# Cross-attention in two stages: all Q of the first batch and the split of the second x in stage one, K loaded ahead of x

## What is computed

```python
qh = _split_heads(x @ wq.T + bq, 16)
kh = _split_heads(ctx @ wk.T + bk, 16)
vh = _split_heads(ctx @ wv.T + bv, 16)
scores = einsum('ntd,nsd->nts', qh, kh) / sqrt(32) + mask * PAD
attn = softmax(scores)
out = _merge_heads(einsum('nts,nsd->ntd', attn, vh)) + x
out = (out - mean) / sqrt(var + 1e-5) * gamma + beta
```

## Time and profile before

| | |
|---|---|
| median of 3 runs | 1111.35 us (1110.16 to 1111.82) |
| profiled execution | 1110.28 us, span 1108.5 us |
| stage one | 0 to 131.4 us of the span |
| steady loop, as read below | 220 to 1000 us |
| busy | PE 97%, DVE 85%, POOL 69%, ACT 65% |

### The profile page before, as it was taken

How to read it: one execution, slowest core, us unless ns; L and a number is a source line. 1 busy time by engine, 2 the same in 40 slices (tenths; PEclk the granted TensorE clock), 3 DMA queues, 4 the chain that set the end, 5 groups by cost and what they waited for, 6 DMA issues and landing times.

```text
span 1108.5 us, 26950 instructions
## 1 busy us (share of the span) xinstructions
PE 1072.9 (97%) x7541; PEld 985.3 (89%) x7541; DVE 939.7 (85%) x1782; ACT 721.0 (65%) x1136; POOL 767.5 (69%) x668
## 2 busy tenths in 40 slices
PE   7999889999999999999999999999999999999984
PEld 6888679999999999999999999999999999999974
DVE  6888478888888888888888888888898888888895
ACT  3321266777777777777777777777777777777651
POOL 3999623576777777777777777777777777777564
PEclk9999999999999999999999999999999999999995
DMA  7754455555655655555556655665665555555443
GB/s 227 257 167 178 171 127 127 133 146 152 167 151 156 164 164 153 141 152 152 136 157 164 164 155 147 154 160 150 160 164 164 140 151 151 144 143 127 126 117 124
DMA packets 176906, 171.34 MB, mean 155 GB/s; under 512 B 110004, under 2 KB 111556, under 8 KB 176868
## 3 DMA queue, kind: packets, MB, share of 16 engines
q1 hardware_dynamic: 167044, 145.36, 45.7%
q10 hardware_dynamic: 9824, 25.50, 10.2%
HBM read 96.76 MB, written 48.85 MB: 131 GB/s over the span
## 4 chain that ended last, share of the span: by engine, by line
PE 82%; DVE 2%; issue 1%; ACT 1%; DMA 1%; SPq 0%; POOL 0%; DVEq 0%; POOLq 0%; ACTq 0%
PE q_ps L811 32%; PE o_ps L859 23%; PE t_ps L845 12%; PE s_ps L831 11%; PE s_ps L834 3%; DMA x_rows<-in_x 1%; PE q_ps L859 1%; SPq L729 0%; DVE attn L950 0%; ACT q_a L1142 0%; DVE stats L919 0%; ACT q_b L1144 0%; POOL attn L1064 0%; DVE row_max L985 0%; ACT pt L1159 0%
## 5 line engine op out<-in xcount | busy, mean ns | idle before, releaser
L859 PE MATMUL o_ps<-v_tiles,pt 128*128 128x66 f32 x2520 | 312.9, 272 | 0.3 <-DVE attn L911 0.3
L859 PEld LDWEIGHTS o_ps<-v_tiles,pt 128*128 128x128 f32 x2520 | 304.3, 193 | 0.5 <-issue 0.5
L1159 ACT COPY pt<-t_ps 128x512 f32<-128x512 f32 (+1 forms) x320 | 186.6, 583 | 159.7 <-PE t_ps L845 156.6
L1096 POOL TENSOR_TENSOR x_lo<-xT_raw,x_hi 128x512 fp32r<-128x512 f32 x124 | 158.2, 1277 | 189.1 <-ACT x_hi L1132 188.6
L985 DVE TENSOR_REDUCE row_max<-s_ps 128x8 f32<-128x616 f32 x256 | 204.7, 800 | 90.0 <-PE s_ps L834 79.1
L1122 ACT ACTIVATE probs<-probs 128x616 f32<-128x616 f32 x256 | 184.3, 720 | 82.3 <-DVE probs L994 74.7
L811 PE MATMUL q_ps<-x_lo,wq_hi 128*128 128x512 f32 x504 | 225.9, 448 | 4.5 <-PEq L148 4.3
L1064 POOL TENSOR_TENSOR attn<-attn,x_rows 128x512 f32<-128x512 f32 x124 | 159.4, 1286 | 94.0 <-DVE attn L911 94.0
L994 DVE TENSOR_TENSOR probs<-s_ps,row_max 128x616 f32<-128x616 f32 x256 | 204.7, 799 | 5.7
L811 PE MATMUL q_ps<-x_hi,wq_hi 128*128 128x512 f32 x504 | 199.5, 396 | 0.0
L811 PE MATMUL q_ps<-x_hi,wq_lo 128*128 128x512 f32 x504 | 199.4, 396 | 0.0
(11 more groups left out here) (96 smaller groups left out, 1666.8 us busy)
## 6 DMA issues: line engine op xcount, KB each, us to landing
xT_raw<-in_xT SPq DMA_DIRECT2D x128, 256.0 KB, 3.4
x_rows<-in_x SPq DMA_DIRECT2D x32, 1024.0 KB, 6.3
out<-y SPq DMA_DIRECT2D x128, 256.0 KB, 2.6
k_scratch<-k_out SPq DMA_DIRECT2D x8, 1232.0 KB, 5.1
k_ac<-k_scratch SPq DMA_DIRECT2D x256, 38.5 KB, 5.5
q_a<-q_a ACTq DMA_DIRECT2D x64, 128.0 KB, 3.1
q_c<-q_a ACTq DMA_DIRECT2D x64, 128.0 KB, 3.5
q_b<-q_b ACTq DMA_DIRECT2D x64, 128.0 KB, 4.1
```

The lines of the kernel that those rows point to most:

```text
L859: mm = pe.matmul(bank_of(b, t)[:, col:col + tile_cols[i]], pt[h][0:w, i, P * t:P * t + P], v_tiles[v_buffer(b, h)][0:w, i, 0:tile_cols[i]] ...
L1096: pool.tensor_tensor(x_lo[par][:, k, :], xT_raw[:, k, :], x_hi[par][:, k, :], ALU.subtract).then_inc(x_lo_ready, 1)
L1159: act.copy(pt[h][0:w, i, :], t_ps[0:w, :]).then_inc(pt_ready, 1)
```

## The change

- The high and low parts of x of batch 1 (`x_hi1`, `x_lo1`) are allocated for both stages and share their memory with `wk_hi` and `wk_lo`, which are free when K of the last chunk is made. ScalarE copies the high parts at the end of stage one; GpSimd subtracts the low parts between its multiplications of the last chunk's values, one behind each of the first four.
- Stage one makes all four groups of Q of batch 0. The PSUM banks are turned (`first_q`), so that groups 2 and 3 lie in the two banks `q_ps` that stage two uses. Groups 0 to 2 are drained in stage one; the moves of groups 0 and 1 are issued ahead of the drain of group 2. Group 3 is drained by ScalarE at the start of step 0, with the moves of groups 2 and 3 behind it, and by VectorE in slot 2 as before.
- In step 0 SyncE issues K of batch 1 first, then gamma and beta, then xT of batch 2. K of batch 1 waits only for the two memsets of its own tiles (`keys_zeroed`), v of batch 0 for the three of the v tiles.
- The waits for gamma and beta stand at their first users.

```diff
@@ allocation
+        x_hi1 = sb(whole, "x_hi1", [P, KC, T], F32R)
+        x_lo1 = sb(whole, "x_lo1", [P, KC, T], F32R)
+        q_ps = [ps(whole, f"q_ps{i}", [P, BANK]) for i in range(2)]
-            wk_hi = sb(one, "wk_hi", [P, KC, D], F32R)
-            wk_lo = sb(one, "wk_lo", [P, KC, D], F32R)
+            wk_hi, wk_lo = x_hi1, x_lo1
-            k_ps = [ps(one, f"k_ps{i}", [P, BANK]) for i in range(NG)]
+            k_ps = q_ps + [ps(one, f"k_ps{i}", [P, BANK]) for i in range(2, NG)]
+            def first_q(g):
+                return k_ps[(g + 2) % NG]
@@ stage one, GpSimd, keep_values
+                        if c == CHUNKS - 1 and j < KC:
+                            pool.wait_ge(x_hi_ready, KC + j + 1)
+                            pool.tensor_tensor(x_lo1[:, j, :], xT_raw[:, j, :], x_hi1[:, j, :], ALU.subtract
+                                               ).then_inc(x_lo_ready, 1)
@@ stage one, ScalarE
+                act.wait_ge(k_done, 2 * NG * CHUNKS)
+                for k in range(KC):
+                    act.wait_ge(xT_loaded[k], 2 * DMA)
+                    act.copy(x_hi1[:, k, :], xT_raw[:, k, :]).then_inc(x_hi_ready, 1)
                 act.wait_ge(consts_loaded, DMA)
-                for g in range(2):
+                for g in range(NG - 1):
+                    if g == 2:
+                        move_first_half()
                     act.wait_ge(q_done, g + 1)
@@ stage one, VectorE: for g in range(2) becomes range(NG - 1)
@@ stage one, TensorE
-                for g in range(2):
+                for g in range(NG):
@@ stage two, SyncE
-                sp.dma_start(gamma_all[:], gamma.partition_broadcast(P)).then_inc(scale_loaded, DMA)
-                sp.dma_start(beta_all[:], beta.partition_broadcast(P)).then_inc(scale_loaded, DMA)
                 def step(a, par):
+                    keys_first = isinstance(a, int) and a == 0
+                    if keys_first:
+                        load_keys(a + 1, 1 - par)
+                        sp.dma_start(gamma_all[:], gamma.partition_broadcast(P)).then_inc(scale_loaded, DMA)
+                        sp.dma_start(beta_all[:], beta.partition_broadcast(P)).then_inc(scale_loaded, DMA)
                     if real(a + 2) and not in_phase_one(a + 1):
@@ load_keys
-                        sp.wait_ge(zeros_set, 5)
+                        sp.wait_ge(keys_zeroed, 2)
@@ stage two, ScalarE, step
+                        if s == 0 and isinstance(a, int) and a == 0:
+                            high_q(0, NG - 1)
+                            move_q(0, 1)
...
-                            if X_STEPS[k] == s and real(a + 2):
+                            if X_STEPS[k] == s and real(a + 2) and not split_in_phase_one(a + 2):
```

More of the change, by code:

```diff
@@ L327, in _ @@
                 pool.wait_ge(wq_lo_ready, 1)
-                pool.wait_ge(x_lo_ready, KC)
+                pool.wait_ge(x_lo_ready, 2 * KC)
             @block.scalar
@@ L350, in keys, with move_first_half @@
                                  ).then_inc(k_hi_copied, 1)
+                def move_first_half():
+                    act.wait_ge(q_hi_ready, 4)
+                    act.dma_start(q_a[QW:P, 0:2, :].bitcast(F32), q_a[0:DH, 0:2, :].bitcast(F32)).then_inc(q_moved[0], DMA)
+                    act.dma_start(q_c[QW:P, 0:2, :].bitcast(F32), q_a[DH:2 * DH, 0:2, :].bitcast(F32)).then_inc(q_moved[0], DMA)
+                    act.dma_start(q_b[0:DH, 0:2, :].bitcast(F32), q_b[QW:P, 0:2, :].bitcast(F32)).then_inc(q_moved[0], DMA)
                 def load_mask():
@@ L528, in _ @@
                 dve.wait_ge(consts_loaded, DMA)
-                for g in range(2):
+                for g in range(NG - 1):
                     dve.wait_ge(q_hi_ready, 2 * g + 2)
-                    dve.scalar_tensor_tensor(out=q_c[0:QW, g, :], in0=k_ps[g][0:QW, :], scalar=bq_col[0:QW, g:g + 1],
+                    dve.scalar_tensor_tensor(out=q_c[0:QW, g, :], in0=first_q(g)[0:QW, :], scalar=bq_col[0:QW, g:g + 1],
                                              in1=q_a[0:QW, g, :], op0=ALU.add, op1=ALU.subtract
                                              ).then_inc(q_lo_ready, 1)
-                    dve.scalar_tensor_tensor(out=q_b[DH:2 * DH, g, :], in0=k_ps[g][QW:P, :],
+                    dve.scalar_tensor_tensor(out=q_b[DH:2 * DH, g, :], in0=first_q(g)[QW:P, :],
                                              scalar=bq_col[QW:P, g:g + 1], in1=q_b[QW:P, g, :],
@@ L598, in _ @@
                 pe.wait_ge(k_masked, 2 * NG * CHUNKS)
-                for g in range(2):
+                for g in range(NG):
                     for k in range(KC):
                         for n, (a, b) in enumerate(terms):
-                            mm = pe.matmul(k_ps[g][:, :], (wq_hi, wq_lo)[a][:, k, P * g:P * g + P],
+                            mm = pe.matmul(first_q(g)[:, :], (wq_hi, wq_lo)[a][:, k, P * g:P * g + P],
                                            (x_hi0, x_lo0)[b][:, k, :], start=(k == 0 and n == 0),
@@ L612, in xattn @@
         zeros_set = sem("zeros_set")
+        keys_zeroed = sem("keys_zeroed")
         scores_done = sem("scores_done")
@@ L637, in xattn @@
         with ExitStack() as two:
-            x_hi = [x_hi0, sb(two, "x_hi1", [P, KC, T], F32R)]
-            x_lo = [x_lo0, sb(two, "x_lo1", [P, KC, T], F32R)]
+            x_hi = [x_hi0, x_hi1]
+            x_lo = [x_lo0, x_lo1]
             k_ac = [k_ac0, sb(two, "k_ac1", [P, 2, NG, 3, SW], F32R)]
@@ L662, in xattn @@
             t_ps = ps(two, "t_ps", [P, BANK])
-            q_ps = [ps(two, f"q_ps{i}", [P, BANK]) for i in range(2)]
             o_ps = ps(two, "o_ps", [P, BANK])
@@ L700, in q_of_step, with in_phase_one, drained_in_phase_one, split_in_phase_one @@
                 return (half + 1) // 2, (0 if half == 1 else 2) + u // 2, u % 2
-            def in_phase_one(b, g=0):
-                return isinstance(b, int) and b == 0 and g < 2
+            def in_phase_one(b):
+                return isinstance(b, int) and b == 0
+            def drained_in_phase_one(b, g):
+                return isinstance(b, int) and b == 0 and g < NG - 1
+            def split_in_phase_one(b):
+                return isinstance(b, int) and b <= 1
             def steps(eng, body):
@@ L725, in load_v @@
                     if isinstance(b, int) and b == 0:
-                        sp.wait_ge(zeros_set, 5)
+                        sp.wait_ge(zeros_set, 3)
                     for i, row, hd, key, n in pieces:
@@ L777, in step @@
                                      ).then_inc(x_loaded, DMA)
-                    if real(a + 1) and not in_phase_one(a + 1):
+                    if real(a + 1) and not in_phase_one(a + 1) and not keys_first:
                         load_keys(a + 1, 1 - par)
@@ L869, in step @@
                         between = [(a - 1 + h, 1 - h, i) for i in TURNS_AHEAD[t]] if real(a - 1 + h) else []
-                        if real(a + ahead) and not in_phase_one(a + ahead, g):
+                        if real(a + ahead) and not in_phase_one(a + ahead):
                             q_half(a + ahead, g, part, (par + ahead) % 2, between)
@@ L935, in scale_row @@
                 def scale_row(b, t, par):
+                    dve.wait_ge(scale_loaded, 2 * DMA)
                     dve.wait_ge(normed, b * 4 + (t + 1))
@@ L1018, in step @@
                             behind = a - 1 if s == 0 else a
-                            if real(behind + ahead) and not in_phase_one(behind + ahead, g):
+                            if real(behind + ahead) and not drained_in_phase_one(behind + ahead, g):
                                 q_low(behind + ahead, g)
@@ L1067, in scale_rows @@
                 def scale_rows(b, t, par):
+                    if t == 0 and (isinstance(b, int) and b == 0):
+                        pool.wait_ge(scale_loaded, 2 * DMA)
                     pool.wait_ge(normed, b * 4 + (t + 1))
@@ L1082, in row_factors @@
                     pool.tensor_tensor(shift[:], neg_mean[:], rstd[:], ALU.mult).then_inc(shift_ready, 1)
[L1084 to L1085 removed]
+                pool.memset(k_ac[1][:].bitcast(F32), 0.0).then_inc(keys_zeroed, 1)
+                pool.memset(k_b[1][:].bitcast(F32), 0.0).then_inc(keys_zeroed, 1)
                 pool.memset(v_tiles[0][:], 0.0).then_inc(zeros_set, 1)
@@ L1182, in step @@
                         ahead, g, part = q_of_step(s)
-                        high = part == 1 and real(a + ahead) and not in_phase_one(a + ahead, g)
+                        high = part == 1 and real(a + ahead) and not in_phase_one(a + ahead)
                         if high:
```

11 lines of the change are left out of this document (2 added, 9 removed).

## The result

The changed kernel takes 1115.36 us (median of 12 runs, 1111.39 to 1120.46); the kernel before, beside it, 1111.90 (12 runs, 1110.16 to 1113.36). The ratio is 1.0029, interval 1.0017 to 1.0041: slower by 3.2 us by the ratio, 3.5 between the medians. The forecast was 1113.8, slower, in 1110.9 to 1116.6. The profiled execution took 1115.09, span 1113.3, against 1108.5: 4.8 more.

A forecast was written before the change was run, and what follows sets the result against it. TensorE, busy 97% of the span, bounds the kernel, so a seam delay carries to the end: +2.1 at the first transposes and +0.4 clock make 1110.28 into 1112.8; with 1.07 for the median, 1113.8, range 1110.9 to 1116.6.

The forecast's parts named there:

- the sum, +2.5: Whole kernel: +2.1 at the first transposes plus +0.4 for the clock, added to the profiled execution's 1110.28.
- 24 matmuls into the barrier hole: TensorE between the stages: Q groups 2 and 3 fill the 4.30 us wait with 5.6 of work, ending at 133.0.
- Release at 134.4: Barrier between the stages: it lets the engines go at 134.4 in place of 131.4, after the added drains.
- Value stores hidden, and the port: End of stage one: last value stores add zero (bound +0.9); GpSimd delays VectorE by at most one instruction, about 1.3.
- the reading that priced 1.1: Shared port, stage one: GpSimd blocks VectorE until its run ends, putting the barrier's release near 135.5; at most 1.1.
- xT issued 9.7 behind the release: SyncE, step 0: memset wait 2.2, K loads to 8.8, gamma and beta to 9.7 after the barrier opens, then xT(2).
- Landing 3.8 after issue, at 13.5: Transfer of xT(2), step 0: lands 13.5 after the barrier opens, with ends 12.2 and 16.7.
- Chain of 4.2 to the mark: ScalarE after xT(2) lands: copy, exp, copy, two activations, exp take 4.1, plus 0.1 to the first transposes.
- TensorE idle 8 to 9.6 ahead of the mark: TensorE ahead of the first transposes: ready about 8 after the barrier opens, then idle 8 to 9.6 us.
- Mark +2.1: Start of TensorE's first transposes, turn(0, 0, 0), behind the seam: 152.1 against 150.04 before, +2.1.
- Clock +0.4: TensorE behind the first transposes: one whole half-clock spell costs 1.7 against 1.3 before, +0.4; bounds 0 to 3.4.
- The rival on the other side: ScalarE in step 0 not held by xT, VectorE sets the first transposes at 144.2: -5.8, 1105.5; chance 0.12.

The follow-up runs named there:

- kernel 1: Changed kernel with SyncE's old order in step 0: gamma and beta, xT of batch 2, then K of batch 1; 1107.48 us, 0.9958 of the kernel before.
- kernel 3: Changed kernel, SyncE's new order kept; in step 0 copies and subtractions of x of batch 2 moved to slots 6, 6, 7, 7; 1107.17 us, ratio 0.9956.
- kernel 2: Changed kernel with gamma and beta issued behind xT of batch 2, K still first; 1111.17 us, 0.9991 of the kernel before.
- kernel 9: As kernel 3 (K first, later copies of x of batch 2), with gamma and beta issued behind v; 1105.51 us, 0.9942 of the kernel before.
- kernel 5: Changed kernel with xT of batch 2 issued first in step 0, then K, v, gamma and beta; 1105.51 us, 0.9939 of the kernel before.
- kernel 4: Kernel before with only SyncE's order changed: K of batch 1, gamma and beta ahead of xT of batch 2; 1113.15 us, ratio 1.0013.
- 7: As kernel 1, but Q groups 2 and 3 of batch 0 made in stage two as before; 1111.38 us, 0.9998 of the kernel before.
- kernel 8: Changed kernel with 42 unused matmuls put ahead of the first transposes; 1114.40 us, 1.0018 of the kernel before.
- 6: As kernel 1, but x of batch 1 split in stage two as before; 1113.26 us, 1.0012 of the kernel before.

## Why the prediction was right

The mechanism was right. The step that decided was read from the lists: K ahead of xT delays a copy that stands ahead of two exponents in ScalarE's order. Kernels 1 and 3 remove it in two different ways, and each turns a loss of 3.2 into a gain of 5. The size was right in part by luck: the sum, +2.5, was a sum over the profiled execution, and between the two profiled executions the change cost 4.8, nearly twice as much; the medians, 3.5 apart, lie nearer to it. Nor did it say "slower" with more than a chance of 0.48. By its steps:

- *24 matmuls into the barrier hole.* Right. The last ends at 132.34 + 0.39 = 132.7, where 133.0 was forecast.
- *Release at 134.4.* It was 133.8. Stage one ran 0.2 earlier in this execution, and VectorE's last instruction (132.74 + 0.76 = 133.5) was followed in 0.28, not 0.67. The 0.67 of the kernel before was counted from the end of an issue of ScalarE; it did not carry over to an instruction of VectorE.
- *Value stores hidden, and the port.* Right. The last value store was issued until 128.75, and from 132 to 133 the DMA engines were busy 0.01 (first stretch above), while VectorE worked until 133.5. VectorE's `low_keys_out` waited for one GpSimd subtraction and no more:

```profile
119.39 1.30 DVE L455 TENSOR_TENSOR k_out<-k_part,k_out 128x308 fp32r<-128x308 f32 x1
```

```profile
119.06 1.30 POOL L317 TENSOR_TENSOR x_lo<-xT_raw,x_hi 128x512 fp32r<-128x512 f32 x1
```

The subtraction ends at 120.36 and VectorE 0.33 later, while GpSimd goes straight on to 128.4; the same operation took 0.46 at 116.81. This agrees with the Trainium skill, "SBUF — State Buffer", section "Who interferes with whom", in its plain sense (one instruction excludes the other), not in the reading that priced 1.1. The 4.43 of the earlier trace rows, longer than any one of the four subtractions beside it, is not explained by it, and no run here looks into it.

- *xT issued 9.7 behind the release.* 10.25: the issue of beta took 1.41 where 0.51 was read from the earlier trace rows; K's issues took 5.99 in place of 6.6.
- *Landing 3.8 after issue, at 13.5.* 5.2 after, at 15.45: the term that was mis-sized, by 1.4, inside its bounds (12.2 to 16.7).
- *Chain of 4.2 to the mark.* 3.95, from 149.23 to 153.18.
- *TensorE idle 8 to 9.6 ahead of the mark.* 10.90: it was ready 8.5 behind the release, about as forecast, and the mark came later.
- *Mark +2.1.* +3.14: -0.6 of the release, +0.55 of the issue, +1.4 of the landing, -0.25 of the chain.
- *Clock +0.4.* The spell behind the mark lasted from 153.18 to 158.94 (0.53 in the slice of 158 means 0.94 at half) and cost 5.76 / 2 = 2.9 against 1.3 before: +1.6. Two spells, the upper bound, would have been 3.4. With this the sum is 3.1 + 1.6 = 4.7.

The spans differ by 4.8, but that the sum comes so near is luck. Behind the mark the kernel before had a hole of 0.40 ahead of its third transposes (155.44), which the changed kernel has not (159.68): there the two are 4.2 apart. The rest is at the end of the kernel, where the steps are unrolled and TensorE has holes. The prediction looked only at the seam; both kernels have about 29 us of half clock there, behind 1080. Kernels 2 and 9 have only 20 and 23. So the half clock differs between executions in a place that the change doesn't touch. The single times of the changed kernel, 1111.39 to 1120.46, go with its mean granted clock (0.985 and 0.977 for these two); which of the two places makes them differ isn't shown, since one execution of each kernel was profiled.

The rival on the other side did not come. Its amount, -5.8, is near what kernels 5 and 1 gave with the wait gone (-6.4 and -5.0), but its terms were not quite those of the runs: their marks came 4.6 and 4.4 sooner than 150.04, not 5.8. The rival had left out what stands ahead of the last exponent in ScalarE's list (two drains in kernel 3, a copy more in kernel 5), and in kernel 1 the fifth score group also waited for the move of Q.

## What to carry to other kernels

Before a transfer is moved behind others on a queue, look at what stands behind its first user in that engine's list: a late load that feeds only the next batch can stop the current one if the instruction that waits for it stands ahead of urgent ones. Then either the transfer goes first or its user goes later; one of the two is enough. A move may also take away the wait that used to hide a late transfer, so each part must be priced in the schedule that the other parts leave. And an idle TensorE cost twice here, by the hole and by the half clock behind it, though filling the hole gave back only part of the second: what is no longer slow can run into the next wait. Last, the engine that a row names for a wait may have been done for long; compare its end with the landings of the transfers before you believe it.

## What the runs showed of the hardware

- Gamma and beta (256 KB each, one row read for all 128 partitions) slow what follows them in the queue. The first piece of xT, issued directly behind them, landed 5.2 after its issue in the changed kernel and 5.5, 5.2, 5.1, 5.0 and 4.7 in kernels 1, 3, 4, 7 and 8; not directly behind them it was 2.5 in the kernel before and 3.5, 2.6, 2.6 and 3.1 in kernels 2, 5, 6 and 9. During 143 to 146 the changed kernel's DMA engines were busy only 0.39 to 0.42. Why is open: no run loads one of them in another form.
- Transfers issued by one engine slow those of another: the last move of Q, issued by ScalarE, landed 2.9 after its issue in the changed kernel, with only K behind the release, 6.3 with xT first (kernel 5) and 7.7 with gamma, beta and xT (kernel 1).
- Behind 12 K loads one of the next issues on SyncE took 1.3 to 1.8 in place of 0.43, whichever it was: beta 1.41 in the changed kernel and 1.81 in kernel 3, a piece of xT 1.60 in kernel 2, 1.31 in kernel 8 and 1.26 in kernel 9. In kernel 4 none did. Its cause is open.
- The half clock that began in the 10.90 hole, 3.0 after TensorE's last matmul, lasted 13.6 us (0.65 in the slice of 145, 0.53 in that of 158), 5.8 of them behind the mark; the one that followed each hole of 4.30 and 2.46 in the kernel before lasted 3.4. In kernel 8, with the hole filled, there was none.
